# The loops of the first and the last block of a four-layer kernel, written out on every engine

## What is computed

```python
x = L0(x, ctx, mask)   # grouped-query cross-attention, 32 heads of 16, 8 kv heads; out @ Wo + x, layer norm
x = L1(x, ctx)         # non-local block: f = phi^T theta, softmax, y = f g, Wz y,
                       #   normalised by mean and variance over batch AND tokens, + x
x = L2(x, ctx)         # RWKV block: layer norm, token shift, a scan over 128 tokens with a 16x16
                       #   state per head, group norm, silu gate, feed-forward
x = L3(x, ctx, mask)   # layer norm, cross-attention with 16 heads of 32, + x, layer norm,
                       #   gelu MLP 512 -> 2048 -> 512, + x
```

## Time and profile before

| what | value |
|---|---|
| median of 3 runs | 4185.63 us |
| lowest, highest | 4185.54, 4189.92 us |
| the profiled execution's own time | 4189.92 us |
| its span in the trace | 4187.9 us |
| its mean granted TensorE clock | 0.981 |
| busy shares PE, PEld, DVE, ACT, POOL | 95%, 60%, 54%, 36%, 34% |
| DMA of instructions (q8, q14) | 279 packets, 4.57 MB; 62 packets, 0.51 MB |

### The profile page before, as it was taken

The page is one execution under the profiler, slowest core; times in us unless marked ns, Lnnn a source line. Parts: engine busy times, 40 slices in busy tenths (PEclk is TensorE's granted clock), DMA queues, the critical chain, the costliest instruction groups (busy, mean ns, idle before and its releaser), DMA issues. The chain is left out here.

```text
span 4187.9 us, 78498 instructions
## 1 busy us (share of the span) xinstructions
PE 3971.5 (95%) x30176; PEld 2492.2 (60%) x30176; DVE 2254.8 (54%) x2705; ACT 1503.1 (36%) x2622; POOL 1405.5 (34%) x1178
## 2 busy tenths in 40 slices
PE   6999999997999999999999999978999999999998
PEld 5666666664666666666666667644544544545443
DVE  3666666664267777766777774325433434434430
ACT  2555555554234434444344433212222322312220
POOL 2333333342254555554554553103121211211210
PEclk8999999998999999999999999988999999999999
DMA  3221222211411001000110002132011010110100
GB/s 102 77 82 65 70 79 79 67 65 66 138 70 51 31 31 41 31 31 31 34 45 33 31 31 83 71 109 109 1 42 37 5 41 3 39 42 1 42 10 10
DMA packets 123637, 212.18 MB, mean 51 GB/s; under 512 B 19296, under 2 KB 39776, under 8 KB 121760
## 3 DMA queue, kind: packets, MB, share of 16 engines
q1 hardware_dynamic: 120736, 200.80, 13.9%
q10 hardware_dynamic: 2560, 6.29, 0.4%
HBM read 125.24 MB, written 67.11 MB: 46 GB/s over the span
## 5 line engine op out<-in xcount | busy, mean ns | idle before, releaser
L2118 PE MATMUL c_pR<-c_proj_w,c_fcT 128*128 128x512 f32 x1024 | 460.0, 597 | 7.2 <-PEq L1965 3.2
L2058 PE MATMUL c_pR<-s_Wfr,c_fc_w 128*128 128x512 f32 x1024 | 458.8, 598 | 5.7 <-ACTq L1965 1.9
L1661 DVE COPY_PREDICATED b_A<-b_mask,b_pS 128x2048 f32<-128x2048 uint32 x96 | 304.4, 3171 | 184.7 <-PE b_pS L1316 183.7
L718 POOL TENSOR_TENSOR a_S<-a_S,a_negmax 128x2048 f32<-128x2048 f32 x64 | 230.9, 3608 | 489.9 <-DVE a_negmax L652 489.9
L1814 POOL TENSOR_TENSOR b_R<-b_R,b_Wh 128x512 f32<-128x512 f32 x192 | 220.1, 1146 | 503.8 <-PE b_pS L1316 503.8
L2058 PEld LDWEIGHTS c_pR<-s_Wfr,c_fc_w 128*128 128x128 f32 x1024 | 191.9, 191 | 246.1 <-issue 241.4
L2118 PEld LDWEIGHTS c_pR<-c_proj_w,c_fcT 128*128 128x128 f32 x1024 | 189.2, 190 | 235.3 <-issue 224.1
L2128 ACT ACTIVATE c_fcT<-c_pR,s_vec 128x512 f32<-128x512 f32 x128 | 88.0, 688 | 609.7 <-PE c_pR L2058 580.9
L2229 DVE TENSOR_TENSOR c_res<-c_res,c_pR 128x512 f32<-128x512 f32 x128 | 88.0, 688 | 399.8 <-PE c_pR L2118 374.9
L2255 POOL TENSOR_TENSOR c_S<-c_S,c_negmax 128x1024 f32<-128x1024 f32 x64 | 121.3, 1895 | 524.3 <-DVE c_negmax L2201 524.3
L1316 PE MATMUL b_pS<-b_R,b_kT 32*128 32x128 f32 x6144 | 228.2, 285 | 42.1 <-POOL b_kT L1819 27.6
(11 more groups left out here) (262 smaller groups left out, 7843.7 us busy)
## 6 DMA issues: line engine op xcount, KB each, us to landing
a_c<-ctx SPq DMA_DIRECT2D x16, 512.0 KB, 4.0
a_x<-x SPq DMA_DIRECT2D x16, 512.0 KB, 5.0
a_kexp<-a_kT SPq DMA_DIRECT2D x512, 16.0 KB, 1.8
mid_cT<-a_cT SPq DMA_DIRECT2D x16, 512.0 KB, 2.6
a_xl<-x SPq DMA_DIRECT2D x32, 256.0 KB, 2.7
a_cl<-ctx SPq DMA_DIRECT2D x32, 256.0 KB, 3.1
mid_x<-a_xl SPq DMA_DIRECT2D x32, 256.0 KB, 3.0
mid_wy<-a_wy SPq DMA_DIRECT2D x32, 256.0 KB, 2.1
```

The lines of the kernel that those rows point to most:

```text
L718: nc.gpsimd.tensor_tensor(S[n % 2][:, :, :], S[n % 2][:, :, :], negmax[n % 2][:, :].unsqueeze(2).to_broadcast([P, RH, T]), ALU.add)\
L1661: nc.vector.copy_predicated(A[:, :, :].rearrange("p q (n two h) -> p q n two h", two=2, h=h)[:, :, :, 1, :], masks[h][:, :].bitcast(U32).r ...
L2058: mm = nc.tensor.matmul(bank, w[:, c, at * P:at * P + P], src[:, c, :], start=(c == 0), stop=(c == KC - 1))
L2118: mm = nc.tensor.matmul(bank, fcT[part % 2][:, m, g * T:g * T + T], proj_w[:, KC * part + m, :], start=(m == 0), stop=(m == KC - 1))
```

## The change

The loops of `phase_a` and of `phase_c` are replaced by Python loops over static turns, on all engines. The steps, their order, their tiles and their handovers stay as they are. Every awaited value and every DMA address in these turns becomes a constant, and the streams of these two blocks hold each turn as its own code.

```diff
@@ phase_a, run (PE, ACT, DVE, POOL); the same edit in its sync block
-            for i in (-1, 0, 1):
-                turn(Turn(None, add=i), i % 2, True)
-            with eng.Fori(0, (N - 4) // 2) as reg:
-                for u in range(2):
-                    turn(Turn(reg, 2, 2 + u), u, False)
-            for i in range(N - 2, N + 2):
+            for i in range(-1, N + 2):
                 turn(Turn(None, add=i), i % 2, True)
@@ phase_c, run
-            turn(Turn(None, add=-1), True)
-            with eng.Fori(0, NG - 1) as reg:
-                turn(Turn(reg), False)
-            turn(Turn(None, add=NG - 1), True)
+            for i in range(-1, NG):
+                turn(Turn(None, add=i), True)
@@ phase_c, sync block
-            turn(Turn(None, add=-1), True)
-            with sp.Fori(0, NG - 2) as reg:
-                turn(Turn(reg), False)
-            for i in range(NG - 2, NG):
+            for i in range(-1, NG):
                 turn(Turn(None, add=i), True)
```

## The result

The changed kernel takes 4164.53 us, the median of 5 runs (4161.14 to 4169.59), against 4185.63 us for the kernel before in the same comparison (4185.23 to 4189.92). The ratio is 0.9948, with a 95% interval of 0.9933 to 0.9962: 21.1 us less. The forecast was 4171 us, 14.6 us less, and its range of 4160 to 4181 holds the result. Later comparisons ran the kernel before again: the medians were 4185.47, 4187.74 and 4186.36 us, with single runs from 4178.55 to 4196.99 us.

The account below looks back on a forecast made before the run. The prediction took PE, busy 95% of the span, as the bound. Savings of 16.3 us in phase_a and 0.6 us in phase_c made 16.9 us; allowing for clock dips in the median run gave 4171 us, range 4160 to 4181.

Parts of the forecast that it names:

- the band of 4165 to 4177 us: Whole kernel: PE's gaps gone and about as many clock dips as before; chance 0.62.
- two guesses on which dips the median run lacked: Median run of before: three fewer dips in phase_b, giving 4168.7 us, or phase_a's three missing, giving 4172.8; middle 4171.
- `phase_a`'s gaps, 12.2 us: PE in phase_a's loop: five idle gaps before sc0 belong to the taken branch and go, 12.2 us.
- The slow clock behind the gaps, 4.2 us: PE in phase_a: three of five gaps are followed by a stretch at 1.2 GHz; 4.2 us go.
- `phase_c`, 0.6 us: PE's 6 back-edges in phase_c: covered by R14 and R15, gain 0.6 us; uncovered they would cost 14.6 us.
- q8 packets: Sign on PE's instruction fetches: already fetched anew each iteration, so written-out code brings about as many packets as before.
- q14 packets, 25 more: Other engines' instruction fetches: phase_a's bodies fetched each time, some 25 more packets, at 0 us on the path.
- Constants, 0: phase_a: constants in place of register values gain 0 us, at most the 4.0 us of waits for ACT.
- Back-edges of the other engines, 0: ACT, DVE, POOL and SP: their back-edges are hidden by slack, so removing them gives 0.
- Slower rival: Small engines' longer code: fetches reach PE's path, 4230 us if all 25 packets are exposed; over 4194 us, chance 0.06.
- The dips of `phase_b`: Rival: phase_b's 6 dips in 12 turns become none (about 4162 us, chance 0.15) or all (4179.5, chance 0.12).
- the short price: Rival that the gap isn't the branch's: at about 108 ns each, 11 back-edges cost 1.2 us, about 4184.4; chance 0.05.

Follow-up runs that it names:

- pe_only: Kernel before with phase_a's loop written out on PE alone, other engines and phase_c keeping their loops: 4162.85 us, ratio 0.9955.
- not_pe: Kernel before with phase_a's loop written out on DVE, ACT, POOL and SP, while PE keeps its loop: 4185.33 us, ratio 1.0000.
- a_regs: Kernel before with phase_a's looped turns written out on all engines, each in a one-iteration loop that keeps register values: 4165.51 us, ratio 0.9949.
- a_four: Kernel before with phase_a's loop at 3 iterations of 4 turns instead of 6 of 2, on all engines: 4174.00 us, ratio 0.9970.
- a_rot: Kernel before with PE's phase_a loop rotated to end behind o0 instead of wy0, same 5 taken branches: 4166.40 us, ratio 0.9948.
- c_only: Kernel before with only phase_c's loops written out, on every engine: 4181.21 us, ratio 0.9990.
- c_rot: Kernel before with PE's phase_c loop rotated so its back-edge stands behind short step p5 instead of R14 and R15: 4204.15 us, ratio 1.0040.
- c_pad: Kernel before with 60 more semaphore increments on PE at the start of phase_c, shifting its loop to touch 7 pages: 4181.91 us, ratio 0.9985.
- c_pad180: Kernel before with 180 more semaphore increments on PE at the start of phase_c, its loop touching 8 pages: 4214.31 us, a single time.
- a_only: Kernel before with only phase_a's loops written out, on every engine; phase_c keeps its own: 4165.10 us, ratio 0.9949.
- all_b: Changed kernel with phase_b's loops written out too, on every engine, so no loop is left: 4180.38 us, ratio 0.9986 to the kernel before.
- rot_pad: Kernel before, all loops kept, with PE's phase_a loop rotated behind o0 and 60 increments before phase_c: 4160.15 us, ratio 0.9945.

## Why the prediction was right, point by point

**The forecast and its sum.** The sum was 16.9 us, the forecast 14.6 us, and 21.1 us were measured: 4164.53 us lies inside the range, but just under the band of 4165 to 4177 us that had most of the chance. The mechanism was right and its size too small. 2.3 us were given away when the forecast was put midway between two guesses on which dips the median run lacked. One of them gave that run none behind `phase_a`'s gaps; the point on the slow clock below shows that the opposite is more likely.

**`phase_a`'s gaps, 12.2 us: right.** The twelve turns took 704.38 us, the sum had 704.7. That the gap is PE's taken branch is shown four ways: by `pe_only` against `not_pe`, by `a_regs`, by `a_four`, and by `a_rot`, which keeps the branches and hides them.

**The slow clock behind the gaps, 4.2 us: the right mechanism, mis-sized.** The prediction took 3 dips, from the one profile of before. Six profiles in which PE's loop of `phase_a` is that of before give 721.01, 720.00, 725.29, 724.79, 726.50 and 728.03 us, with 3, 2, 6, 6, 7 and 8 dips of 1.4 us (order: `before`, `c_only`, `not_pe`, `c_rot`, `c_pad`, `c_pad180`). Their mean is 724.3, which is 19.9 us over 704.4, not 16.3. With `phase_c`'s 2 us this makes 21.9 us, and 21.1 us were measured. A number that changes from run to run had been taken from one run.

**`phase_c`, 0.6 us: too small.** Only recorded waits were counted. The turns were 163.77 us with PE "busy" throughout, but 163.55 us when written out, so 0.2 us per turn of the stall stood inside what is shown as busy. From `n1` to the sixth `n2` it is 1.8 us, over all back-edges about 2 us. The cover was there, as read: branches of 6.3 us end about where the 7.03 us of `R14` and `R15` do, and without that cover 5 of them cost 21.4 us (`c_rot`), slow clock included, where the prediction put 14.6 us on 6.

**q8 packets "about as before": wrong.** A pair of turns of `phase_a` brings 9, not 11, and the whole program 254, not 279. The trace of before records 2413 instructions of PE in a pair, that of the changed kernel 2336: 118 register instructions and the branch are gone, and 42 semaphore instructions more stand there. That is 0.3 of a packet; the rest is that straight code isn't fetched twice at a branch. That "PE's code is too long to be kept" holds for `phase_a` (2413 instructions) and not for `phase_c`, where it hangs on 7 or 8 pages. So writing out `phase_c` was worth nothing once `phase_a` was written out: `a_only` has that 2 us already.

**q14 packets, 25 more: half right.** They came in every pair of `phase_a`'s turns, but 18 in the twelve turns where there had been 5, so 13 more and not 25; `phase_c`'s block had 12 more. The total went only from 62 to 64, since `phase_b`, untouched, had 16 where it had had 43. By likeness to `phase_c` its loops lie differently in the pages; that was not tried.

**Constants, 0: right** (`a_regs`), though not for the reason given: the trace does record register instructions, on the sequencers. The 118 of a pair on PE take 32 to 50 ns each, with no idle time of PE to show for them. **Back-edges of the other engines, 0: right** (`pe_only`, `not_pe`); in the trace of before their taken branches last 45 to 74 ns. **Slower rival: ruled out in `phase_a`** by `not_pe`; `all_b` shows that written-out code can be slower in another block. **The dips of `phase_b`:** as many in the two profiles, 6 of 12 turns. **The rule on the branch's own length** in the Trainium skill ("Advanced Engine Details and Errata", Control Flow Timing, about 108 ns) lies a little above a branch of PE that isn't taken (67 to 94 ns here) and is half of a taken one whose target is held (215 ns). For the others the trace agrees with the Trainium skill's section Instruction fetch mechanics ("Runtime: NRT & Kernel Launch"): a packet of 0.9 to 1.2 us came within each of `phase_a`'s five branches of 3.3 to 3.8 us. It doesn't agree with that section's window of two pages, as `phase_c`'s loop was held on PE when it touched 7. By the short price alone the change would have come out at no difference.

## What to carry to other kernels

Look up the loop's branches by their source line first: their duration less the matmul time already issued behind them is the price of a back-edge, to within 0.5 us. If it is too high, end the loop behind a step whose work outlasts the branch, which was as good here as writing it out and needs hardly more code. Don't expect written-out code to be faster as such: in the middle block it was 16 us slower. Where PE is the bound, add the slow clock behind each gap, taken over several profiles; and after any change of code size look again at the loops that follow, as they may be held or fetched anew by where they lie.

## What the runs showed of the hardware

- A taken back-edge on PE's sequencer took 3.3 to 3.9 us when the loop's code was fetched anew (one in `rot_pad` 4.4 us), 0.22 to 0.24 us when it was held, and a branch not taken 0.07 to 0.09 us. Behind `R14` and `R15` of `phase_c` it took 6.2 to 6.8 us in four kernels (`before`, `not_pe`, `a_rot`, `c_pad180`), where the packet within it started 3 us later, for a reason that stays open.
- By the offsets of the compiled streams, a loop of 1708 instructions on PE was held when it touched 7 pages of 16 KB (`a_only`, `c_pad`, `a_four`, `a_regs`, `pe_only`, `rot_pad`) and fetched anew, 8 or 9 packets per turn, when it touched 8 (`before`, `not_pe`, `a_rot`, `c_rot`, `c_pad180`).
- An idle time of 2.2 to 2.8 us on PE was followed by a stretch at 1.2 GHz in some runs after 2 of 5 gaps and in others after all 5, at 1.4 us each or twice that. In `a_rot`, where no gap is left, the twelve turns had no such stretch.
